# Pair adds of an attention moved from GpSimd to VectorE, and the evictions' engines exchanged

## The reference

```python
xn = _layernorm(x)
s = _L0_attn_ref(xn, ...)            # causal, 16 heads of 64, output projection, layer norm
# the DAG of six nodes:
for c in range(6):
    nsrc = min(c + 1, 5); snode = c - nsrc
    q = ew[c, 0] * (nodes[c - 1] @ We[lind + nsrc - 1] + be[...])
    k = ew[c, 1] * (nodes[snode] @ We[lind] + be[...])
    v = ew[c, 2] * (nodes[snode + nsrc // 2] @ We[lind + nsrc // 2] + be[...])
    # o: 8 heads of 128, projections Wq, Wk, Wv; softmax over all 2048 keys, not causal; Wo
    o = _mha(q, k, v, Wq[c], Wk[c], Wv[c], Wo[c])
    nodes[c] = act_w[c] * o + q
    lind += nsrc
g = silu(_layernorm(nodes[5]))
out = x + s * g
```

## Time and profile before

| What | us |
|---|---|
| median of the runs (9651.75 to 9657.07) | 9654.41 |
| profiled execution | 9646.32 |
| its span, slowest core (the eight: 9588.6 to 9644.8) | 9644.8 |
| busy in that span: TensorE matmul | 6523.3 |
| busy: ScalarE | 2766.9 |
| busy: GpSimd | 1985.1 |
| busy: VectorE | 1660.9 |

### The profile page before, as it was taken

The page is one execution under the profiler, slowest core; times in us unless marked ns, Lnnn a source line. Parts: engine busy times, 40 slices in busy tenths (PEclk is TensorE's granted clock), DMA queues, the critical chain, the costliest instruction groups (busy, mean ns, idle before and its releaser), DMA issues.

```text
span 9644.8 us, 62523 instructions; the slowest of 8 cores (9588.6 to 9644.8 us)
## 1 busy us (share of the span) xinstructions
PE 6523.3 (68%) x21827; PEld 2053.0 (21%) x21827; DVE 1660.9 (17%) x2300; ACT 2766.9 (29%) x2612; POOL 1985.1 (21%) x1122
## 2 busy tenths in 40 slices
PE   0766677666696665976667866669666587887860
PEld 0211123111241111321112311114211132111110
DVE  2111111111111111111111111111111112222235
ACT  0233322333213333123332133331333222333321
POOL 0222222222212223122222122231222310000000
PEclk9877788777797777987778977779777787555565
DMA  3100022000140001310002200013000121000013
GB/s 99 46 0 0 0 70 70 0 0 0 40 118 18 0 0 31 109 35 0 0 0 66 92 0 0 0 31 109 18 0 0 31 57 31 0 0 0 0 32 90
DMA packets 204570, 289.39 MB, mean 30 GB/s; under 512 B 141576, under 2 KB 141800, under 8 KB 204268
## 3 DMA queue, kind: packets, MB, share of 16 engines
q1 hardware_dynamic: 204236, 285.39, 10.0%
q0 software_dynamic: 32, 0.00, 0.0%
HBM read 218.24 MB, written 33.55 MB: 26 GB/s over the span
## 4 chain that ended last, share of the span: by engine, by line
PE 60%; POOL 18%; DVE 9%; issue 5%; DMA 5%; ACT 2%; SPq 1%; DVEq 0%; POOLq 0%; ACTq 0%
POOL attb L615 17%; PE ps L384 14%; PE ps L564 9%; PE ps L869 7%; PE ps L634 6%; PE ps L625 6%; PE ps L610 6%; PE ps L447 4%; DVE stat L515 3%; PE ps L595 3%; PE ps L586 3%; PE ps L508 2%; DVE attb L499 2%; DMA fio<-x 1%; DMA wstage<-fWe 1%
## 5 line engine op out<-in xcount | busy, mean ns | idle before, releaser
L675 ACT ACTIVATE attb<-ps,negM,scal 128x1024 bf16<-128x1024 f32 x1536 | 1798.1, 1201 | 3297.4 <-PE ps L625 1608.6
L615 POOL TENSOR_TENSOR attb<-attb 128x1024 bf16<-128x1024 bf16 x768 | 1623.4, 2114 | 3912.8 <-PE ps L610 3898.1
L625 PE MATMUL ps<-attb,ones_bf 128*1 128x512 bf16 x1536 | 562.2, 454 | 1584.5 <-POOL attb L615 1584.5
L384 PE MATMUL ps<-slot,wbuf 128*128 128x512 bf16 x6144 | 1365.2, 383 | 218.9 <-POOL wbuf L358 197.8
L564 PE MATMUL ps<-qbuf,kbuf 128*128 128x512 bf16 x3072 | 1299.5, 523 | 136.0 <-ACT attb L675 120.9
L384 PEld LDWEIGHTS ps<-slot,wbuf 128*128 128x128 bf16 x6144 | 604.0, 99 | 966.2 <-issue 255.9
L869 PE MATMUL ps<-slot,wbuf 128*128 128x512 bf16 x3072 | 746.1, 405 | 81.6 <-POOL wbuf L358 81.6
L358 POOL CAST wbuf<-wstage 128x1024 bf16<-128x1024 f32 x344 | 360.1, 1051 | 2040.6 <-DMA wstage<-fWe 938.2
L610 PE MATMUL ps<-attb,slot 128*128 128x512 bf16 x1536 | 670.7, 532 | 35.5 <-DVE slot L737 35.5
L508 PE MATMUL ps<-attb,ones_sq 128*128 128x512 bf16 (+1 forms) x512 | 238.9, 565 | 609.4 <-DVE attb L499 608.2
L732 DVE CAST wb_sb<-ps 128x1024 bf16<-128x1024 f32 (+1 forms) x128 | 156.3, 1221 | 2800.5 <-PE ps L723 2800.5
(11 more groups left out here) (101 smaller groups left out, 2943.5 us busy)
## 6 DMA issues: line engine op xcount, KB each, us to landing
wstage<-fWe SPq DMA_DIRECT2D x120, 512.0 KB, 4.3
wstage<-fWv SPq DMA_DIRECT2D x48, 512.0 KB, 4.1
wstage<-fWq SPq DMA_DIRECT2D x48, 512.0 KB, 4.1
wstage<-fWk SPq DMA_DIRECT2D x48, 512.0 KB, 4.2
wstage<-fWo SPq DMA_DIRECT2D x48, 512.0 KB, 4.2
slot<-n_sp SPq DMA_DIRECT2D x40, 512.0 KB, 8.1
fio<-x SPq DMA_DIRECT2D x32, 512.0 KB, 4.0
n_sp<-slot SPq DMA_DIRECT2D x32, 512.0 KB, 2.7
```

Of the source, the lines that this page charges most:

```text
L384: t.matmul(ps[pb][:, sg * SEG:(sg + 1) * SEG], wtile(ws, kc, do * 128, 128), fchunk(ss, kc, th * TW + sg * SEG, SEG), start=(kc == 0), sto ...
L615: t_pr = P.op("gpsimd", lambda v, a0=a0, a1=a1: v.tensor_tensor(attb[a0][:, 0:PW], attb[a0][:, 0:PW], attb[a1][:, 0:PW], ALU.add), waits=[ ...
L625: t.matmul(ps[3][0:1, o:o + w], ones_bf[:, 0:1], attb[a0][:, o:o + w], start=first, stop=last),
L675: off=off: s.activation(attb[ab][:, off:PW], ps[pb][:, off:PW], AF.Exp, bias=negM[:, nc_:nc_ + 1], scale=scale_col),
```

## The change

Two edits. In `projection`, ScalarE now evicts the odd row blocks and VectorE the even ones. In `pair_a`, the in-place add of the two exponential tiles is issued to VectorE's queue instead of GpSimd's, with the same waits; its completion is counted on VectorE's semaphore, which is what L625 and the second buffer's release then wait for.

```diff
@@ -400,7 +400,7 @@
                 slot_read(src_slot, t_mm)
-                eng = "scalar" if do % 2 == 0 else "vector"
+                eng = "scalar" if do % 2 == 1 else "vector"
 
                 def ev_s(s, do=do, th=th, pb=pb, ds=dst_slot, TW=TW):
@@ -612,9 +612,9 @@
                     v_tile_fn(kc0), attb[a0][:, o:o + w],
                     start=first, stop=False, tile_position=tp),
                     waits=[r0] + ([ps_last[2]] if j0 == 0 else []), inc="tPE")
-            t_pr = P.op("gpsimd", lambda v, a0=a0, a1=a1: v.tensor_tensor(
+            t_pr = P.op("vector", lambda v, a0=a0, a1=a1: v.tensor_tensor(
                 attb[a0][:, 0:PW], attb[a0][:, 0:PW], attb[a1][:, 0:PW],
-                ALU.add), waits=[r0, r1, t_av0], inc="tPOOL")
+                ALU.add), waits=[r0, r1, t_av0], inc="tDVE")
```

## The result

| What | before | after |
|---|---|---|
| profiled execution, us | 9646.32 | 7832.19 |
| span of the slowest core, us | 9644.8 | 7830.7 |
| granted clock, mean over that core's span | 0.763 | 0.841 |
| busy, us: GpSimd | 1985.1 | 364.4 |
| busy, us: VectorE | 1660.9 | 2200.7 |

The ratio of after to before is 0.8092, with a 95% interval of 0.8066 to 0.8117: 9653.9 us became some 7812. That is faster by more than was forecast (8000, with a range from 7850 to 8300).

A forecast was written before the change was run, and what follows sets the result against it. The bound was taken to be a ring between TensorE and GpSimd's add. Gains of 1488 (add and clock), 34 (warm projection) and 143 (head 7), less 12 (casts), make 1653 us: 9646.3 becomes about 8000, range 7850 to 8300.

The forecast's parts named there:

- What bound it: In the attention pairs, GpSimd's add and TensorE's matmuls form a ring; a turn takes 4.40 us, with TensorE waiting 1.77.
- The add's term: The pair add L615 goes from 2114 ns on GpSimd to 692 on VectorE: 768 x 1.42 = 1091 us at constant clock.
- The clock, second term: In the attention tiles, less TensorE waiting keeps the clock up; 1488 us gained over 48 heads, the add's 1091 included.
- Six turns of 2.98: Within each query tile, six full-clock turns between L625s at 2.98 us each, 17.88 together.
- 2.87 for the last step: At a query tile's end, the step between the last two L625 falls from 4.29 us to 2.87.
- plus 1.5 for the low clock's overhang: Second query tile of a head: 1.5 us (0.9 of a turn) added for a spell at the lower clock.
- 120.0 each: Time per head before the change, from heads 1 to 7 of a node starting 719.96 us apart in six steps.
- Head 7: In each node's head 7, adds no longer queue behind 16 GpSimd weight casts: 6 x 23.9 = 143 us gained.
- Casts and adds side by side: In head 7, GpSimd casts can hold VectorE adds: 12 us lost, at worst 102.
- The evictions: In the projections, exchanging ScalarE's and VectorE's output rows is worth zero, within 5 us either way.
- The case without overhang: Likeliest case's fast end: no low-clock spell at the starts of tiles, 120 us less, 7880 us.
- the rivals: Four: clock stays (8432, 0.14); ScalarE bounds (8065, 0.06); no gain (about 9650, 0.02); slower, clock pulled down (0.02).

The follow-up runs named there:

- turns of 3.5 us: Kernel after the change with one extra VectorE pass of the add's form per pair, results unused; profiled execution 8341.5 us, fastest 8316.0.
- VectorE's step of 1.89 us: Kernel after the change with two extra VectorE passes of the add's form per pair, results unused; ratio to before 0.9252, about 8935 us.
- one of 2.16: Kernel after the change with two extra full VectorE passes and one of 384 columns per pair; profiled execution 9612.1 us, fastest 9603.7.

## Why the prediction fell short

**What bound it: right.** The add's ring between GpSimd and TensorE was the bound. Moving the add alone gives the whole result.

**The add's term: right.** 2114 ns became 692 in the median, the 692 to 693 that the earlier trace rows gave; the expected 0.35 us of wait per turn came out as 0.31, the expected 400 us in all as 354.

**The clock, second term: the mechanism was right, and here the prediction failed.** It had been argued only from which turns were slow. The additional matmuls show it: at an unchanged add, they alone take 6.5% off the time. The step that failed is the size of this term: 1488 + 34 us for 48 heads, or 31.7 per head, of which 1091 is the shorter add at constant clock. Measured are 35.3 us in the mean of heads 0 to 6. Above the 1091, the forecast left 431 us for the clock and the tile ends; on the same footing the runs show some 600 (an estimate, 48 x 35.3 - 1091), close to the 620 us that four more matmuls gave the old kernel through the clock. What the forecast had wrong is how long a head's tiles stay at the lower clock, what their last step takes at full clock, and how long the average head was before; the list below has each.

The working of the two tiles can be held against the trace of after. Here are the last two L625 of a first tile, its Ln, the Ln that ends the second tile, and from the head behind it the first exponential and the first L625:

```profile
2622.07 0.59 PE L625 MATMUL ps<-attb,ones_bf 128*1 128x512 bf16 x2 [0.94 <-DVE attb L615]
...
2624.58 0.59 PE L625 MATMUL ps<-attb,ones_bf 128*1 128x512 bf16 x2 [0.95 <-DVE attb L615]
...
2625.27 1.01 ACT L710 ACTIVATE fio<-ps 1x1024 f32<-1x1024 f32 x1 [3.14 <-PE ps L625]
...
2653.84 1.01 ACT L710 ACTIVATE fio<-ps 1x1024 f32<-1x1024 f32 x1 [3.14 <-PE ps L625]
...
2683.70 2.30 ACT L675 ACTIVATE attb<-ps,negM,scal 128x1024 bf16<-128x1024 f32 x2 [27.61 <-DVE negM L531]
...
2688.96 1.01 PE L625 MATMUL ps<-attb,ones_bf 128*1 128x512 bf16 x2
```

and that head's first Ln:

```profile
2710.66 1.01 ACT L710 ACTIVATE fio<-ps 1x1024 f32<-1x1024 f32 x1 [3.14 <-PE ps L625]
```

- "Exponential to first L625: 5.40": measured 2688.96 - 2683.70 = 5.26. "Ln to first L625: 7.78" is 7.75, from 2625.27 to 2633.02. Right.
- "Six turns of 2.98": 2.94 or less. "2.87 for the last step": 2624.58 - 2622.07 = 2.51. I took the 4.29 us between the last two L625 from a tile's end whose matmuls were partly at the lower clock (1.01 us for the second L625), and carried it into a sum for the full one. With the six turns it is 0.6 us per tile, about 58 us in all.
- "Plus 1.0" and "plus 1.5 for the low clock's overhang": the steps without overhang add up to 5.26 + 17.6 + 2.5 + 0.7 = 26.1 in the first tile and 7.75 + 17.6 + 2.5 + 0.7 = 28.6 in the second. In the rows above the first takes 2710.66 - 2683.70 = 26.96 and the second 2653.84 - 2625.27 = 28.57. One head says little here, since the overhang comes and goes. In the mean of the 36 heads 1 to 6 (from the starts of L675 and L710 in the timeline) the tiles take 26.37 and 29.13 us, an overhang of some 0.3 and 0.6 for the forecast 1.0 and 1.5. That is 1.6 us per head, 77 us in 48, and the larger part of the error.
- Together the tiles take 55.5 us for the forecast 58.6.
- "120.0 each" was read in one node, the shortest. The mean of the 36 heads before is 121.0; this alone hid 0.95 us per head, 46 us in 48. The same goes for the clock: 0.78 was read in one head, and the mean over the two tiles is 0.73 in those 36 heads, with 0.78 at the top.
- One slip went the other way. The 89.6 us before run to the start of the next head's projection, but the 58.6 end at Ln, 0.87 us earlier (3031.15 to 3032.02); the gain came out 0.9 us per head too high by that. It didn't show, because the stretch from Ln to the first exponential also shrank by more than the 0.8 that had been forecast: from 3062.43 - 3031.15 = 31.3 us to 2683.70 - 2653.84 = 29.9. By luck the two nearly cancel.

Heads 0 to 6 gained 1481 us where 42 x 31.7 = 1332 had been forecast; the six heads 7 with all that follows them 336 for 6 x (31.7 + 23.9) - 12 = 322; and the start lost 3. That makes the 161 us between forecast (1653) and traces (1814).

**Head 7: right.** The queue's wait is gone; the wait for an add is 1.3 us at most in after. The forecast was 143 us, from the longest of the six first waits, 25.92 us (the others have 23.4 to 25.3). Measured, heads 7 and what follows gain 336 - 6 x 35.3 = 124 us more than other heads, with the price of the casts in it (143 - 12 = 131 forecast). **Casts and adds side by side: right in kind and size**, and seen in both directions. In a head 7 of after:

```profile
2943.85 1.04 POOL L358 CAST wbuf<-wstage 128x1024 bf16<-128x1024 f32 x1 [1.57 <-DMA wstage<-fWo]
...
2946.55 1.04 POOL L358 CAST wbuf<-wstage 128x1024 bf16<-128x1024 f32 x1 [1.67 <-DMA wstage<-fWo]
...
2947.12 1.02 DVE L615 TENSOR_TENSOR attb<-attb 128x1024 bf16<-128x1024 bf16 x1 [4.51 <-PE ps L610]
...
2957.18 0.69 DVE L615 TENSOR_TENSOR attb<-attb 128x1024 bf16<-128x1024 bf16 x1 [2.25 <-PE ps L610]
2957.20 1.57 POOL L358 CAST wbuf<-wstage 128x1024 bf16<-128x1024 f32 x1 [1.36 <-DMA wstage<-fWe]
...
2959.97 1.04 POOL L358 CAST wbuf<-wstage 128x1024 bf16<-128x1024 f32 x1 [1.21 <-DMA wstage<-fWe]
...
2960.12 1.44 DVE L615 TENSOR_TENSOR attb<-attb 128x1024 bf16<-128x1024 bf16 x1 [2.25 <-PE ps L610]
```

The add at 2947.12 took 1.02 us, and the one at 2960.12 1.44, both begun during a cast; each ended 0.55 us after the cast did (2947.59, 2961.01). The cast at 2957.20, begun behind an add, took 1.57 instead of 1.04. The mean of all adds is 698 ns, 6 above the median: 5 us in 768, for which 12 stood in the sum. The Trainium skill ("SBUF — State Buffer", who interferes with whom) says that of such a pair whichever starts first keeps the shared ports for its whole instruction and the other is held. The trace agrees in the order and for both engines. It doesn't show that the held add does nothing meanwhile: it ends 0.55 us behind the cast, where a whole add takes 0.69.

**The evictions: right as far as can be measured**, nothing within 0.3% (29 us); the forecast 5 us can't be told from zero.

**The range.** The case without overhang gave 7880, and the range ended 30 us below it, at 7850. But that case was built on the same 2.87, 2.98 and 120.0. A bound must be built of bounds: every term of the case "full clock throughout" should have been taken from rows at full clock. The granted clock over a head's two tiles, forecast above 0.9, is 0.92 in the mean of the 36 heads; the 0.88 above is that of whole heads. None of the rivals came true: the clock followed, 763 of the 768 adds start on the heels of L610, and TensorE's wait in a turn is still for the add and not for an exponential.

## What to carry to other kernels

When TensorE waits a little in every turn of a loop, look whether the granted clock suffers, and if so count the wait twice: once for itself, and once for the matmuls that run at 1.2 GHz because of it. Here that was so in turns of 4.40 us with 1.77 of waiting; with 0.91 of waiting in turns of 3.5 us the clock over the heads was 0.88, as in turns of 2.93. Before moving work between engines, look whether the bounding engine's queue also holds slower things ahead (here 16 casts fed by DMA), and try whether a matmul or two of padding lifts the clock: one of 512 columns per pair took 5% off. Whoever sums a case at full clock must take every row from a stretch at full clock, and whoever multiplies a head by 48 must look at more than one node first.

## What was not expected of the hardware

How steeply the granted clock falls. With VectorE's step of 1.89 us (turns of 4.14) the clock over heads 1 to 6 was 0.83, with one of 2.16 (turns of 4.48) 0.72; 0.34 us more per turn cost some 670 us, over twice its own 261. One more matmul per pair lifted the clock from 0.75 to 0.86 at the same turn of 4.40. And VectorE's add on 1024 bf16 columns takes 692 ns alone, while in a row each further one adds 0.6 us.
